# Weight maxima through TensorE, context sizes inside the expert loop, weight scales ahead of attention

## What is computed

```python
x = x + _L0_xattn_ref(_layernorm(x), itok, ctx)          # x @ ctx[itok]^T per position
x = x + _L0_ffn_ref(_layernorm(x), w_red, wg, W1, b1, W2, b2)   # 8 experts, top 1
x = x + _L1_xattn_ref(_layernorm(x), ctx, ctx, mask, Wq, bq, Wk, bk, Wv, bv, Wo, bo)
x = x + _L1_ffn_ref(_layernorm(x), gate_w, up_w, down_w, s_in, s_in_down)

def fp4_global_scale(w):
    return FP8_MAX * FP4_MAX / jnp.max(jnp.abs(w))       # one maximum per weight matrix
def fake_quant_nvfp4(x, global_scale):                   # blocks of 16
    amax = jnp.max(jnp.abs(xb), axis=-1, keepdims=True)
    sc = jnp.clip(amax / FP4_MAX * global_scale, 0.0, FP8_MAX)
    dq = sc.astype(float8_e4m3fn).astype(float32) / global_scale
    q = jnp.sign(xb) * _FP4_VALS[jnp.digitize(jnp.clip(abs(xb) / dq, 0, 6), _FP4_MIDS)]
    return (q * dq).reshape(sh)
```

## Time and profile before

| | us |
|---|---|
| median of 3 runs (lowest to highest) | 811.22 (810.25 to 811.69) |
| the profiled execution: its time | 805.57 |
| its span, first to last instruction | 803.8 |
| busy: PE / DVE / ACT / POOL | 634.5 / 603.4 / 409.1 / 209.9 |
| share of the chain that ended last: PE / DVE / ACT / issue | 50% / 21% / 13% / 9% |

### The profile page before, as it was taken

How to read it: one execution, slowest core, us unless ns; L and a number is a source line. 1 busy time by engine, 2 the same in 40 slices (tenths; PEclk the granted TensorE clock), 3 DMA queues, 4 the chain that set the end, 5 groups by cost and what they waited for, 6 DMA issues and landing times.

```text
span 803.8 us, 14057 instructions
## 1 busy us (share of the span) xinstructions
PE 634.5 (79%) x3943; PEld 464.5 (58%) x3944; DVE 603.4 (75%) x1551; ACT 409.1 (51%) x709; POOL 209.9 (26%) x256
## 2 busy tenths in 40 slices
PE   6495889259999999868799999999644666676665
PEld 3383667137766677557678888887511433344334
DVE  5283677866766767745897889888749898989995
ACT  1341323123323333247465666665785788777772
POOL 6526354524555445410111222201100000000000
PEclk9697888769999999969799999999976778877998
DMA  8784344361211220060000000000000000000001
GB/s 320 257 329 147 105 164 173 105 230 57 70 49 60 59 69 34 25 210 2 1 0 0 0 0 0 0 0 2 2 3 0 12 15 27 13 26 13 26 26 53
DMA packets 30958, 53.99 MB, mean 67 GB/s; under 512 B 4973, under 2 KB 23806, under 8 KB 29760
## 3 DMA queue, kind: packets, MB, share of 16 engines
q1 hardware_dynamic: 24480, 39.02, 14.5%
q0 software_dynamic: 5568, 13.61, 4.9%
q10 hardware_dynamic: 864, 0.82, 0.3%
HBM read 39.38 MB, written 15.93 MB: 69 GB/s over the span
## 4 chain that ended last, share of the span: by engine, by line
PE 50%; DVE 21%; ACT 13%; issue 9%; another core or an unknown queue 2%; DMA 2%; SPq 2%; DVEq 1%; ACTq 0%; POOL 0%; POOLq 0%
PE quad L1150 9%; PE bank L1167 8%; PE quad L1099 6%; PE bank L1287 4%; PE quad L1271 3%; PE bank L1302 2%; PE bank L1484 2%; PE quad L1452 2%; ACT ctxs L982 2%; PE quad L1158 2%; ACT hqT L999 2%; DVE nS L2020 2%; PE quad L1461 2%; DMA ctxs<-in_ctxT 2%
## 5 line engine op out<-in xcount | busy, mean ns | idle before, releaser
L1150 PE MATMUL quad<-W1s,xts 128*128 x160 | 74.7, 607 | 0.3 <-DVE hid L1781 0.3
L1167 PE MATMUL bank<-W2s,hidT 128*128 x320 | 72.5, 379 | 0.3 <-ACT hidT L730 0.3
L1484 PE MATMUL bank<-dT,hqT 128*128 128x256 bf16 x256 | 50.3, 369 | 27.2 <-ACT hqT L999 27.2
L606 POOL TENSOR_TENSOR X<-fo,X 128x256 f32<-128x256 f32 (+1 forms) x32 | 21.9, 683 | 175.9 <-DVE fo L2042 155.7
L1167 PEld LDWEIGHTS bank<-W2s,hidT 128*128 128x128 f32 x320 | 60.0, 190 | 12.6 <-issue 5.3
L726 ACT ACTIVATE hid<-hid 128x512 f32<-128x512 f32 x40 | 25.3, 633 | 76.2 <-DVE hid L1781 76.2
L1287 PE MATMUL bank<-nVB,nPT 128*128 128x34 f32 x512 | 63.0, 279 | 0.0
L1287 PEld LDWEIGHTS bank<-nVB,nPT 128*128 128x128 f32 x512 | 59.6, 191 | 3.7
L555 POOL DMA_INDIRECT x_after_ffn<-row,niU x40 | 39.4, 984 | 71.5 <-DVE row L1793 54.0
L2195 DVE SCALAR_TENSOR_TENSOR hh<-quad,gmx,sil 128x512 f32<-128x512 f32 x64 | 45.1, 745 | 12.8 <-PE quad L1461 6.0
L1484 PEld LDWEIGHTS bank<-dT,hqT 128*128 128x128 bf16 x256 | 32.2, 132 | 38.5 <-ACT hqT L999 29.3
(11 more groups left out here) (326 smaller groups left out, 1502.8 us busy)
## 6 DMA issues: line engine op xcount, KB each, us to landing
row<-rows_by_expert SPq DMA_DIRECT2D x38, 134.0 KB
W1s<-in_ctxO SPq DMA_DIRECT2D x4, 1024.0 KB, 7.8
...
```

What stands on the lines that cost most here:

```text
L1150: ins = pe.matmul(bank[2 + u % 2][:], xt[:, u, c, :], W1s[:, bass.ds(ex, 1), c, :].rearrange("p o s -> p (o s)"), start=c == 0, stop=c == ...
L1167: ins = pe.matmul(bank[6 + u % 2][:, 0:D], hidT[:, u % 2, c, :], W2s[:, bass.ds(ex, 1), c, :].rearrange("p o s -> p (o s)"), start=c == 0, ...
L1484: ins = pe.matmul(bank[(1, 7)[u // 2]][:, (u % 2) * D:(u % 2 + 1) * D], hqT[:, u % 2, c, :], dT[:, c, :], start=c == 0, stop=c == FT - 1)
```

## The change

Three things. (1) The three weight maxima become columns 7 to 9 of `bound` and cross the partitions with the bound's own two transposes; the second one now reads the column of maxima broadcast, so that every partition gets all ten. `weight_maxima` and POOL's all-reduce go. (2) `context_size` is taken in the loop: four batches of context in each of the three h = 0 groups, two and two in the last group (`context_size(k, n, to)` reads n batches from k * n on, so `context_size(2 * NTR, 2, 3)` reads batches 12 and 13 into column 3, and the other one 14 and 15); both weight sizes of the last group move up by one `outs`, and the three column maxima stand ahead of `outs(3)`. (3) `weight_scales` and `weight_rounding` run ahead of the batches, `weight_inverses` in batch 1, `inverse_rows(2)` stays in 2, `activation_scales` runs in 3. The diff, without the declarations of the three tiles that grow to ten columns and of the two semaphores that go:

```diff
@@ gpsimd
-            def weight_maxima():
-                pool.wait_ge(s_wmx, 1)
-                pool.partition_all_reduce(gmx[:, 3:6], gmx[:, 0:3], P, bass.bass_isa.ReduceOp.max).then_inc(s_war, 1)
...
                 context(2)
-                weight_maxima()
                 batch(1, p=2)
@@ tensor
-            pe.transpose(bank[6][0:8, 0:P], bound[:], ident[:]).then_inc(s_bndT, 1)
+            pe.transpose(bank[6][0:10, 0:P], bound[:], ident[:]).then_inc(s_bndT, 1)
             pe.wait_ge(s_bnd, 2)
-            pe.transpose(bank[6][0:1, P:P + 8], boundm[:], ident[0:8, 0:8]).then_inc(s_bndT, 1)
+            pe.transpose(bank[6][:, P:P + 10], boundm[:].broadcast_to([10, P]), ident[0:10, 0:10]).then_inc(s_bndT, 1)
@@ vector
-            def context_size(n, b0, b1):
-                red(boundc[:, n:n + 1], ctxs[:, b0:b1, :, 0:S].rearrange("p b c s -> p (b c) s"), AX.XY, ALU.max,
+            def context_size(k, n, to=None):
+
+                red(boundc[:, bass.ds(k, 1)] if to is None else boundc[:, to:to + 1],
+                    ctxs[:, bass.ds(k * n, n), :, 0:S].rearrange("p b c s -> p (b c) s"), AX.XY, ALU.max,
                     apply_absolute_value=True)
@@ experts
                 else:
-                    context_size(1, NB // 2, NB // 2 + 2)
+                    context_size(2 * NTR, 2, 3)
                 hidden(3)
                 if last:
-                    context_size(2, NB // 2 + 2, NB // 2 + 4)
+                    context_size(2 * NTR + 1, 2, 4)
                 outs(0)
                 if not last:
                     next_scores(g + 1, (h + 1) % 3)
                 else:
-                    context_size(3, NB // 2 + 4, NB // 2 + 6)
+                    weight_sizes(PARTS - 2, st)
                 outs(1)
                 if last:
-                    context_size(4, NB // 2 + 6, NB)
+                    weight_sizes(PARTS - 1, st)
                 elif h:
                     v.wait_ge(s_wr, 16 * 3)
                     weight_sizes(i * 2 + (h - 1), st)
+                else:
+                    context_size(i, 4)
                 outs(2)
                 if last:
-                    weight_sizes(PARTS - 2, st)
+                    for n in range(3):
+                        red(bound[:, 7 + n:8 + n], sizes[:, spans[n]], AX.X, ALU.max)
                 outs(3)
-                if last:
-                    weight_sizes(PARTS - 1, st)
-
-            context_size(0, 0, NB // 2)
+
             next_rows(0, 0, 0)
@@ bound
-            red(boundm[:], bank[6][0:8, 0:P], AX.X, ALU.max).then_inc(s_bnd, 1)
+            red(boundm[:], bank[6][0:10, 0:P], AX.X, ALU.max).then_inc(s_bnd, 1)
             v.wait_ge(s_bndT, 2)
-            st.link(v.tensor_copy(boundA[:], bank[6][0:1, P:P + 8]))
+            st.link(v.tensor_copy(boundA[:], bank[6][:, P:P + 10]))
@@ weight_scales
-                v.wait_ge(s_war, 1)
-                steps.link(v.reciprocal(gmx[:, 3:6], gmx[:, 3:6]))
+                steps.link(v.reciprocal(gmx[:, 3:6], boundA[:, 7:10]))
@@ attention
                 st.need()
-                weight_maxima()
                 inverse_rows(0, stn)
                 v.wait_ge(n_bo, 1)
                 tt(boS[:], boS[:], bank[7][:, 0:D], ALU.add).then_inc(n_fo, 1)
+                weight_scales(stn)
                 keys_in(0, 0, 0)
                 inverse_rows(1, stn)
+                weight_rounding(stn)
                 masked(0, 0)
...
-                def second():
-                    inverse_rows(2, stn)
-                    weight_scales(stn)
-
-                batch(1, 1, 1, first=True)
-                batch(2, 0, 1, between=second)
-                batch(3, 1, 2, between=lambda: weight_rounding(stn))
-                batch(4, 0, 2, between=lambda: weight_inverses(stn))
-                batch(5, 1, 3, between=lambda: activation_scales(stn))
+                batch(1, 1, 1, first=True, between=lambda: weight_inverses(stn))
+                batch(2, 0, 1, between=lambda: inverse_rows(2, stn))
+                batch(3, 1, 2, between=lambda: activation_scales(stn))
+                batch(4, 0, 2)
+                batch(5, 1, 3)
```

15 lines of the change are left out of this document (4 added, 11 removed).

## The result

The changed kernel takes **807.73 us** as a median (799.45 to 813.08, 22 runs), the one before, in as many runs beside it, 811.24 us (802.97 to 817.56). The ratio is **0.9942, 95% interval 0.9919 to 0.9965**: by it 4.7 us less, between 2.8 and 6.6 (the two medians alone differ by 3.5). Forecast were 803.4 us and a gain of 7.8. The profiled execution took 800.04 us with a span of 798.3; the span before was 803.8.

What follows compares the result with a forecast made beforehand. Limits were taken to differ by stage, PE carrying half the span and DVE a fifth. Terms -1.4 + 0.4 - 1.6 - 5.2 = -7.8 us took the 811.22 us median to 803.4 us, range 799.5 to 808.3.

Steps and rivals of the forecast that it cites:

- Head of the loop: Start of the expert loop: without `context_size(0)` DVE waits only for the first rows, -1.4 us (ends -1.7 and -0.8).
- In the loop: Expert loop: a four-batch context reduction in each of three h = 0 groups, +0.4 us in all (ends 0 and +6.6).
- It just about fits: Expert loop: a reduction of about 2.2 us against DVE waits of 0.91, 0.45 and 0.90 us, together 2.26.
- Last group and flag: Loop's last group: fewer context reductions and earlier weight sizes bring the bound at 340.4 instead of 342.07, -1.6 us.
- The pause: Pause ahead of the batches: weight scales and rounding hidden behind DVE's waits for ACT and PE, cost 0; uncovered 3.3 us.
- Batches 1 to 5: First attention batches: stall gone, weight work moved; 14.8, 16.3, 12.4, 13.5, 12.0, sum 69.0 against 74.2 us, -5.2.
- Rival 1: Attention: the 7.0 us belong to POOL's first add, so the stall stays; gain only 3.8, 807.4 us; chance 0.08.
- Rival 2: Attention: ACT's wait only followed the stall, so batch 2 falls to 13.5 us; total -10.6, 800.6 us; chance 0.15.
- Rival 3: Expert loop: late DVE idles PE and lowers its clock in three passes; +4.1 us, 815.3 us; chance 0.03.

Runs made afterwards that it cites:

- before_bound_maxima: The kernel before with only the weight maxima moved onto the bound and the all-reduce removed, order of work unchanged; ratio 0.9934 to the kernel before.
- after_roots_early: The changed kernel with ACT's row-scales wait moved to its first user and the last rows' square roots put mid-batch 1; ratio 0.9883 to the kernel before.

## Why the prediction was right, and where it was not

*The direction and the range hold.* 807.73 us lies in 799.5 to 808.3, 0.6 us from its slow end. The gain of 7.8 us was too large against 4.7 (2.8 to 6.6). The median was taken as 0.7% above the profiled execution; it is 1.0% above. The two spans differ by 5.5 us, and the two rows of the account that lie outside all terms (-2.39 and +2.73) nearly cancel.

*Head of the loop, -1.4.* Right in kind: -0.87 here, within its ends. On the other chips, where the rows landed sooner, the head fell by 2.0 to 2.7 us in the versions that put nothing in it, beyond the end of -1.7. In some profiles part of that came back as a longer first interval, in others the first interval was shorter too.

*In the loop, +0.4: this term failed.* It was +2.6: 2.2 in the eight later intervals and 0.4 in the first, with its lower clock. PE's waits for `hid` show 1.8 of it. The step that failed is "It just about fits": I set 2.2 us against waits of 2.26 although I had said that the last of them holds the loading of an expert number. That load is 0.76 us of "issue" in the row at 189.18, so only 0.91 + 0.45 + (0.90 - 0.76) = 1.50 us were free, which leaves 2.29 - 1.50 = 0.79 without cover. The intervals behind the three reductions grew by 0.80, 0.70 and 0.68 us, while PE's waits for `hid` were 0.75, 0.44 and 0.45. Doubling the work, halving it by place and taking it out agree (the table of intervals above). The measured case is between my end of 0 and that of 6.6.

*Last group and flag, -1.6:* measured -1.71, the same in all eleven profiles of the new form (28.79 to 28.85). The wider transposes cost nothing (flag 2.59 us behind the fold, before 2.61). *The pause, 0:* right. The row of the account, +0.03, holds batch 0 as well, and runs with the same code have 28.2 to 32.2 us there; nearly all of this spread is batch 0, 11.1 to 15.0 us at a granted clock of 1.00 to 0.75. From the folding to the first `masked` it is 13.7 to 13.9 us in the three profiles of the old form and 13.3 to 14.2 in the eleven of the new. In all eleven DVE still waits, 0.63 to 1.52 us for ACT ahead of `nKB` and 0.85 to 1.29 us for PE ahead of `nS`, so the work is covered.

*Batches 1 to 5, -5.2:* measured -5.93, each batch within 0.4. The total hides that two reasons were wrong, and that it is partly luck. I gave batch 4 a gain of 3.0 for the inverses; they cost 1.5, and the rest was a dip of the clock that before_bound_maxima does not have. And I kept batch 2 long because of ACT's wait for the row scales; with that wait gone the batch did not change, and with the table loads moved it did. The length came out right because I carried over a measured 16, not because the reason held. And 14.8 and 16.3 fit one of two forms of batches 1 and 2; the other has 13.32 and 17.00.

*Rival 1* (the stall stays) is refuted twice: no switch in the changed kernel, and the 7 us movable by one instruction. *Rival 2* (batch 2 at its steady pace) did not happen, but 13.27 us can be had. *Rival 3* (slower by the loop) did not decide at 2.29 us; at 4.4 us it does, about where I had put the point (4.2 us).

*Against the Trainium skill.* GpSimd needs 8.0 to 10.0 us before an all-reduce here, and 6.8 to 7.0 to return; the Trainium skill's GPSIMD Engine Reference, section 2.1, has about 6 for a first call, so the trace does not agree. The 8.8 us of the first run hold no wait for the input, whose last column DVE had written by 346.5, 5 us before the switch began. Nor does the trace agree with section 4 of the GPSIMD Engine Reference of the Trainium skill, by which GpSimd is the only option for a reduction across partitions: the two transposes gave the maxima of three more columns within the time that they had taken before.

*Open:* the rest of the program has 255.3 to 255.6 us in five profiles, 257.3 to 258.5 in five, and 259.2 to 261.2 in four, with the same instructions. One execution of each kernel was profiled, so whether the change itself makes the longer form likelier was not settled. It does not by need: after_roots_early has the short one. The start of the feed-forward part, before and then after:

```profile
588.50:608.50 20.00, 7.21 (x29) 2.31 (x27) 12.53 (x22) 17.57 (x24) 0.00 (x0) 0.76 0.00 1
```

```profile
580.30:600.30 20.00, 9.27 (x29) 3.04 (x27) 11.07 (x22) 17.67 (x24) 0.00 (x0) 0.67 0.00 0
```

PE is busy 2.1 us longer for the same 29 matmuls, at a granted clock of 0.67 for 0.76. If this is booked as chance, the change is worth -5.8 us on the first chip (all rows of the account but the first and the last), and 1.7 of that is the dip of the clock in batch 4 before.
